# The one-hot's targets as 16-bit integers: a second-layer broadcast is read from a table that the first stage casts on chip

## The reference

```
# layer 0: attention with 4 heads of 32
xl = x @ W_lin.T;  ef = edge_attr_16 @ W_edge.T
alpha = leaky_relu(sum(xl[dst]*att_src) + sum(xl[src]*att_dst) + sum(ef*att_edge))
alpha = softmax of alpha over the edges of one dst
out   = segment_sum(xl[src] * alpha, dst) + bias + x;  out = elu(layernorm(out)*gamma + beta)
x     = layernorm(x + out)
# layer 1: 8 heads of 16, no softmax
q, k, v = x @ Wq.T, x @ Wk.T, x @ Wv.T
alpha = sum(q[dst] * w * k[src], by head) / 4 * cutoff        # w is edge_attr_128
out   = segment_sum(alpha * v[src], dst);  x = layernorm(x + out)
```

## Time and profile before

| what | us |
|---|---|
| median of 3 runs (4947.43 to 4953.25) | 4952.8 |
| the profiled execution's own time | 4959.02 |
| its span, first to last instruction | 4957.3 |
| POOL busy in the span | 3076.0 |
| DVE busy | 2651.6 |
| PE busy | 2132.6 |

### The profile page before, as it was taken

How to read it: one execution, slowest core, us unless ns; L and a number is a source line. 1 busy time by engine, 2 the same in 40 slices (tenths; PEclk the granted TensorE clock), 3 DMA queues, 4 the chain that set the end, 5 groups by cost and what they waited for, 6 DMA issues and landing times. The chain is left out here.

```text
span 4957.3 us, 48938 instructions
## 1 busy us (share of the span) xinstructions
PE 2132.6 (43%) x10968; PEld 1744.4 (35%) x10968; DVE 2651.6 (53%) x5053; ACT 264.3 (5%) x645; POOL 3076.0 (62%) x3266
## 2 busy tenths in 40 slices
PE   2344545444444544444444443443443344433443
PEld 1233334333333433333333333333333333333333
DVE  2344454444445444444546666666666666666665
ACT  1000000000000000000010000000000000000000
POOL 5666666666666666666516666666666666666665
PEclk6566667666666666666665555555555555555555
DMA  6334443433444343344326655665566666665664
GB/s 148 103 101 112 111 108 106 111 100 100 111 113 108 106 109 103 100 109 114 93 90 190 193 183 187 189 184 180 184 185 191 185 190 186 189 186 181 188 187 130
DMA packets 373356, 711.83 MB, mean 144 GB/s; under 512 B 129400, under 2 KB 216744, under 8 KB 373048
## 3 DMA queue, kind: packets, MB, share of 16 engines
q0 software_dynamic: 130384, 326.81, 25.0%
q1 hardware_dynamic: 197896, 354.70, 22.3%
q10 hardware_dynamic: 45024, 29.80, 1.9%
HBM read 682.88 MB, written 28.15 MB: 143 GB/s over the span
## 5 line engine op out<-in xcount | busy, mean ns | idle before, releaser
L532 POOL DMA_INDIRECT ring<-x_table,idx x1612 | 1524.6, 946 | 916.4 <-issue 461.1
L1211 POOL DMA_INDIRECT ring<-kv_table,den_cols x1520 | 1436.7, 945 | 780.0 <-issue 448.5
L1253 PE MATMUL psum<-work,ring 128*128 128x42 f32 x3232 | 736.8, 419 | 429.5 <-DVE ring L1379 209.7
L1253 PEld LDWEIGHTS psum<-work,ring 128*128 128x128 f32 x3232 | 705.9, 330 | 483.2 <-issue 325.1
L1245 PE MATMUL psum<-ring,work 126*128 126x128 bf16 x1616 | 206.7, 308 | 986.5 <-DVE ring L1368 607.0
L633 PE MATMUL psum<-work 128*42 128x132 f32 x3232 | 598.6, 361 | 43.9 <-DVE work L930 30.0
L633 PEld LDWEIGHTS psum<-work 128*42 128x42 f32 x3232 | 489.4, 160 | 120.0 <-DVE work L930 40.4
L1245 PEld LDWEIGHTS psum<-ring,work 126*128 126x128 bf16 x1616 | 155.9, 139 | 1018.4 <-issue 783.3
L1365 DVE TENSOR_TENSOR psum<-psum,ring 128x1024 f32<-128x1024 f32 x202 | 248.2, 1229 | 450.2 <-issue 263.6
L942 DVE TENSOR_TENSOR sumT<-sumT,psum 128x42 f32 x202 | 40.2, 199 | 606.7 <-PE psum L641 565.2
L830 DVE TENSOR_TENSOR work<-dst_all,psum 126x1024 bf16<-126x1024 int32 x204 | 249.2, 1222 | 165.9 <-DMA dst_all<-dst_row_dram 94.1
(11 more groups left out here) (201 smaller groups left out, 2170.5 us busy)
## 6 DMA issues: line engine op xcount, KB each, us to landing
dst_all<-dst_row_dram SPq DMA_DIRECT2D x406, 512.0 KB
ring<-ea_dram SPq DMA_DIRECT2D x202, 512.0 KB
ring<-x_table,idx POOLq DMA_INDIRECT x1612
ring<-kv_table,den_cols POOLq DMA_INDIRECT x1520
ea_pair<-ea_turned_dram SPq DMA_DIRECT2D x102, 128.0 KB
kv_table<-work ACTq DMA_DIRECT2D x17, 512.0 KB
q_table<-work ACTq DMA_DIRECT2D x17, 384.0 KB
ring<-q_table SPq DMA_DIRECT2D x202, 31.5 KB
```

What stands on the lines that cost most here:

```text
L532: pool.indirect_dma_start(x_rows[:, h * CHUNK_TILES + t, :], None, k["x_table"], bass.IndirectOffsetOnAxis(idx[h][:, t:t + 1], 0))\
L1211: pool.indirect_dma_start(kv[j][:, t, :], None, k["kv_table"], bass.IndirectOffsetOnAxis(index[:, tile:tile + 1], 0))\
L1253: last = pe.matmul(sum_ps[j % 2], message[j % 2][:, t, :], onehot[j][:, t, :], start=t == 0, stop=t == GROUP - 1)
```

## The change

The targets in `dst_row` are int32 numbers from 0 to 6250. In the first stage the changed kernel loads them once, as 128 rows of 1632 numbers, into free columns of `ring`. DVE casts them to int16, and SP writes them to a new table `dst_half` in device memory. The broadcast of the second layer reads that table, and DVE's comparison in the second layer reads int16. The first layer still broadcasts int32. The buffers `dst_all` keep their size; the second layer uses half of their columns, seen as int16.

```diff
+    dst_half = nc.dram_tensor("dst_half", [1, TILES0 * P], I16, kind="Internal").ap()
...
+    dst_line = ring[:, at:at + TILES0].bitcast(I32)
+    at += TILES0
+    dst_short = ring[:, at:at + TILES0 // 2].bitcast(I16)
...
@@ first stage, SP
                 sp.dma_start(xT_sb[:, pieces], xT[:, pieces]).then_inc(xT_in[i], 16)
+            sp.dma_start(dst_line, dst_row.rearrange("o (p n) -> (o p) n", p=P)).then_inc(line_in, 16)
...
             sp.wait_ge(ai_split, 1)
             sp.dma_start(ai_table.rearrange("(b p) s h -> p b (s h)", p=P), ai_parts.rearrange("p b s h -> p b (s h)"))\
               .then_inc(ai_out, 16)
+            sp.wait_ge(line_cut, 1)
+            sp.dma_start(dst_half.rearrange("o (p n) -> (o p) n", p=P), dst_short).then_inc(line_out, 16)
             sp.wait_ge(ai_out, 16)
             sp.wait_ge(rows_out, 16 * PIECES)
+            sp.wait_ge(line_out, 16)
@@ first stage, DVE
             last.then_inc(ai_split, 1)
+            dve.wait_ge(line_in, 16)
+            dve.tensor_copy(dst_short, dst_line).then_inc(line_cut, 1)
@@ layer1
-    dst_all = k["dst_all"]
+    dst_all = [t[:, 0:GP // 2].bitcast(I16) for t in k["dst_all"]]
...
-                    sp.dma_start(dst_all[j % 2], k["dst_row"][0:1, bass.DynSlice((SLOTS * i + j) * GP, GP)]
+                    sp.dma_start(dst_all[j % 2], k["dst_half"][0:1, bass.DynSlice((SLOTS * i + j) * GP, GP)]
                                  .to_broadcast([P, GP])).then_inc(dst_in[j % 2], 16)
```

More of the change, by code:

```diff
@@ L19 @@
 I32 = mybir.dt.int32
+I16 = mybir.dt.int16
 ALU = mybir.AluOpType
@@ L169, in program @@
     ai_parts = ring[:, at + 2 * AI:at + 4 * AI].bitcast(BF16)[:, 0:3 * AI].rearrange("p (b s h) -> p b s h", s=3, h=HEADS0)
+    at += 4 * AI
+    dst_line = ring[:, at:at + TILES0].bitcast(I32)
+    at += TILES0
+    dst_short = ring[:, at:at + TILES0 // 2].bitcast(I16)
+    at += TILES0 // 2
+    line_in = S("line_in")
+    line_cut = S("line_cut")
+    line_out = S("line_out")
     ai_made = S("ai_made")
@@ L187, in program @@
     LOADS = ((0, 1), (1, 3), (3, PIECES))
-    assert PIECES * PIECE_NODES == NODE_ROWS and at + 4 * AI <= RING_COLS
+    assert PIECES * PIECE_NODES == NODE_ROWS and at <= RING_COLS
     pair_ps = [psum[:, (2 + j) * 512:(2 + j) * 512 + 2 * W0] for j in range(PIECE_PAIRS)]
@@ L321, in program @@
         x_table=x_table, ai_table=ai_table, q_table=q_table, kv_table=kv_table, xpad=xpad,
-        src_idx0=src_idx0, src_tile=src_tile, dst_row=dst_row, dst_runs=dst_runs, ea_turned=ea_turned,
+        src_idx0=src_idx0, src_tile=src_tile, dst_row=dst_row, dst_half=dst_half, dst_runs=dst_runs, ea_turned=ea_turned,
         ea=ea, ew=ew, x1_table=x1_table, fin_sb=fin_sb, rows_sb=rows_sb, w_sb=w_sb, neg_ident_bf=neg_ident_bf, out=out, ident_sb=ident_sb, iota_sb=iota_sb,
```

## The result

The changed kernel takes 4967.05 us (median of 14 runs, 4963.12 to 4975.53), the kernel before, run beside it, 4956.98 us (14 runs, 4947.43 to 4967.06). The ratio is 1.0022, 95% interval 1.0015 to 1.0029: 10 us slower, where 20 us of gain less 4 us were forecast. The profiled execution of the changed kernel is the slowest of its 14 (4975.53 us), so the profiles lie further apart (16.5 us) than the medians.

What follows compares the result with a forecast made beforehand. The prediction took POOL's issue of gathers, with its waits, to bound the kernel. From a median of 4952.8 us, plus 4 for the first stage, less 20 in the second layer, it forecast 4936.8 us, 8 in 10 for 4880 to 4975.

Steps and rivals of the forecast that it cites:

- The bound: Second layer: POOL's issue of gathers, 1905 of 2257 us, with its waits, bounds the kernel; DVE does not.
- First stage, +4 us, between 0 and 8: First stage: loading the targets adds 2.5 us and writing `dst_half` 1.5, so the stage grows by 4 us.
- The cast: First stage: DVE's cast of the targets to int16 takes 1.8 us, hidden before the next stage starts.
- The comparison at 1.22 us: Second layer: DVE's comparison with int16 stays at 1.22 us, a change of 0 with 10 us to each side.
- 53 MB less: Second layer: SP's queue moves 53 MB less, from 202 broadcasts each 0.26 MB smaller.
- So I count half of the waits, with half of the time each: 44 x 0.46 = 20 us: Second layer: sooner landings shorten 44 of POOL's 88 waits for PE's signal by 0.46 us each, gaining 20 us.
- no gain: Rival: the second layer gains nothing and only the first stage's 4 us count: 4957 us, chance 0.28.
- only 14.9 us are named waits for a landing: Second layer, argument for no gain there: POOL's waits named as for a landing total only 14.9 us.
- A new rhythm of waits, slower: Rival, POOL's wait at t = 6: 101 waits in place of 88, up to 43 us more, 5000 us, chance 0.17.
- The rhythm breaks the other way: Rival, POOL's waits for PE's signal: half of them go, 145 us less, 4812 us, chance 0.05.
- The forecast's own range: Whole kernel: 4870 to 4943 us, for a gain of 10 to 82 us in the layer, less 4; chance 0.50.
- The 2 us and 436 GB/s: A DMA's fixed cost and byte rate from a skill page; by them each broadcast saves 0.6 us, gaining 13 us, not 20.

Runs made afterwards that it cites:

- b_again: The kernel before, unchanged, run again beside the kernel before at 4960.45 us: 4958.75 us, ratio 0.9996.
- a_again: The changed kernel, run again beside the kernel before at 4960.45 us: 4970.69 us, ratio 1.0019.
- stage_only: The kernel before plus the first stage's load, cast and write, second layer's broadcast still int32: 4233.46 and 4229.25 us, ratios 1.0007 and 1.0003.
- e7: The changed kernel with every second group's sums signalled only during the next group's sums, against the kernel before: 5055.82 us, ratio 1.0188.
- e4_before_free: The kernel before without POOL's wait for the sums at t = 6, against the kernel before at 4229.76 us: 4227.02 us, ratio 0.9994.

## Why the prediction was wrong

- **The bound.** Right: POOL's issue and its waits. The account of the change by gather starts closes to 0.2 us with the waits at t = 6 and for landings alone.
- **First stage, +4 us, between 0 and 8.** Inside the bounds and too high: 1.4 us in the profile, 3.9 us between b_again and a_again, 1 to 4 us in stage_only. The cast was put at 1.8 us and took 1.00, hidden.
- **The comparison at 1.22 us.** Right: 1221 ns.
- **53 MB less.** Right: 51.7.
- **The failing step: "So I count half of the waits, with half of the time each: 44 x 0.46 = 20 us".** It took for granted that PE's signal follows the landing. A group that lands sooner does start its messages sooner (402.7 us of idle time in place of 433.9), but the signal isn't on that chain: in the timeline above it is 9 us behind its last matmul, and comes when POOL has stood for 2.9 us. The waits at t = 6 came to +23 to +31 us, not -20, with their mean length 0.3 to 0.4 us up. The "no gain" rival had the reason, that PE's signal may have one of its own, and had 0.28.
- **Where the gain lay.** The step "only 14.9 us are named waits for a landing" put it aside as small. By gather starts it is 26.0 us (15.4 in b_again), and it is all the change can give: 13.5 to 24.7 us on the late level, 10 on the prompt one.
- **"A new rhythm of waits, slower".** Nearest to what happened, with 0.17. Its rhythm came, a wait in every second group (95 of 101 waits after 16 gathers, 45 of 105 before), and so did its sign. Its price didn't: it wanted 13 more waits, and there are 90 in place of 88 by the view, 101 in place of 105 by gather starts. What changed is which lengths they have.
- **"The rhythm breaks the other way"** rested on late signals from the load on the DMA engines. The prompt level has more load and none of them.
- **The forecast's own range** was given as 4870 to 4943 us. A gain of 10 to 82 us less the stage's 4 is 4875 to 4947: the 4 us were left out. It changes nothing above.
- **The 2 us and 436 GB/s** come from a section of the Trainium skill ("DMA: Bandwidth & Descriptors", "Anatomy of one DMA — SWDGE (gpsimd) path") on transfers that POOL issues; the broadcast is SP's. No run here shows a fixed part for it, and the sum didn't use one.
- The measured 4967 us is nearest to the 4957 of "no gain" and lies inside the range of 4880 to 4975, 30 us over the forecast. That it does is the range's width; the direction was wrong.

What stays open is why int16 makes landings be told later in e7, how the loss divides between the second layer and what lies ahead of it, and what sets the level. That gathers and signals compete for one path on the late level fits the traces, but no run shows the path, and the recording is a rival that no run excludes.

## What to carry to other kernels

Account for a wait by where the bounding engine stands in its loop, not only by the releaser that a view names: the sum of two positions gave this layer to 0.2 us, and showed a gain and a loss that the totals blurred. Sort the waits by what went before them as well: the mean wait grew by 0.4 us here, and among waits with equally many gathers ahead of them the median stood still. A wait for another engine's signal is only shortened by earlier work if the signal follows that work; compare the end of the producing instruction with the moment at which its consumer goes on before counting on it. And a change of 0.2% can have either sign by the level that an execution falls into (0.998 for int16 in the second layer alone, 1.002 for it and for the whole change), and a pacing wait can be worth nothing or 8% (0.9994 and 1.079 without it): keep such a wait until it has been tried on both levels.

## What the runs showed of the hardware

- The same kernel takes 4227 to 4230 us or 4957 to 5032 us, with PE's granted clock at 0.60 and 0.58. In the slower case most records of semaphore changes are missing (7434 of 25856 for the gathers' landings in the first trace; 25843 in e4_before_free). The second layer is 2029 or 2355 us, the first 2128 or 2531, so 326 and 403 us of the difference.
- At the slow end a semaphore increment of PE is late in half of the groups and more (by 6.6 us in the median before, 8.5 after), and some issues of SP take 0.70 us in place of 0.35, while POOL issues gathers without a break. The increment comes some 2 to 3 us after POOL stops, and the stop costs POOL 1.9, 2.7, 3.3 or 4.2 us after 8, 10, 16 or 24 gathers. At the other end neither occurs, with more bytes per second (215 GB/s against 183).
- Taking away one pacing wait of POOL changed nothing that could be measured at one end (0.9994, 0.9997) and cost 397 us at the other.
- A DVE cast of 1632 int32 columns to int16 took 1.00 us; the comparison of 1024 columns took 1.22 us with int16 as with int32.
